# A decoder layer on one core: attention's value products for two key blocks at a time, and the last key block added to the sum by VectorE

## The reference

```python
qkv = x @ w_qkv + b_qkv                                   # self: 16 heads of 32
scores = einsum('bhqd,bhkd->bhqk', q, k) / sqrt(32)
scores = where(causal, scores, -10000.0)                  # cross: where(mask, -inf, scores)
probs = softmax(scores)
ctx = einsum('bhqk,bhkd->bhqd', probs, v)
x = x + ctx @ w_dense + b_dense
...
x = x + cross_attention(layernorm(x), ctx_1024, mask)
x = x + experts(layernorm(x))                             # argmax of 8, gelu between two 512x512 products
```

## Time and profile before

| | |
|---|---|
| Three timed runs | 1970.99, 1971.99, 1972.17 us |
| The profiled execution | span 1969.3 us (the page gives no other time of it) |
| PE busy | 1878.3 us, 95% of the span |
| PE weight loads busy | 1325.4 us, 67% |
| VectorE busy | 1349.2 us, 69% |
| ScalarE busy | 1128.1 us, 57% |
| GpSimd busy | 975.0 us, 50% |
| Mean granted TensorE clock | 0.981 |

### The profile page before, as it was taken

The page is one execution under the profiler, slowest core; times in us unless marked ns, Lnnn a source line. Parts: engine busy times, 40 slices in busy tenths (PEclk is TensorE's granted clock), DMA queues, the critical chain, the costliest instruction groups (busy, mean ns, idle before and its releaser), DMA issues. The chain is left out here.

```text
span 1969.3 us, 34918 instructions
## 1 busy us (share of the span) xinstructions
PE 1878.3 (95%) x10950; PEld 1325.4 (67%) x10950; DVE 1349.2 (69%) x2849; ACT 1128.1 (57%) x2168; POOL 975.0 (50%) x1144
## 2 busy tenths in 40 slices
PE   6999999999999999999999999999999875899997
PEld 4667777777777766666666666666666454798896
DVE  5667667676766676667676757576665476788886
ACT  3555555555555555555565656565555444688885
POOL 3455456445555555455454445554454442355454
PEclk9999999999999999999999999999999886999999
DMA  6455554645555573644444545535353456722220
GB/s 186 120 142 126 131 133 97 148 108 119 116 138 132 130 187 88 140 109 110 102 112 108 129 108 123 114 91 125 87 113 81 103 191 197 266 67 93 84 89 17
DMA packets 137658, 239.18 MB, mean 121 GB/s; under 512 B 31066, under 2 KB 32386, under 8 KB 137440
## 3 DMA queue, kind: packets, MB, share of 16 engines
q1 hardware_dynamic: 108704, 190.49, 35.5%
q0 software_dynamic: 21392, 45.37, 11.6%
q10 hardware_dynamic: 7408, 1.42, 0.4%
HBM read 114.84 MB, written 48.97 MB: 83 GB/s over the span
## 5 line engine op out<-in xcount | busy, mean ns | idle before, releaser
L558 ACT ACTIVATE attn_probs<-attn_sT 128x512 f32<-128x512 f32 (+3 forms) x1024 | 528.6, 518 | 475.8 <-PE attn_sT L872 472.8
L466 POOL TENSOR_TENSOR attn_probs<-attn_probs 128x512 f32<-128x512 f32 (+2 forms) x384 | 531.2, 1402 | 179.1 <-PE attn_o_ps L887 130.4
L667 DVE TENSOR_REDUCE attn_m_col<-attn_sS 128x1 f32<-128x512 f32 x512 | 342.7, 688 | 194.2 <-PE attn_sS L856 186.5
L872 PE MATMUL attn_sT<-attn_stack 98*128 98x512 f32 (+2 forms) x1024 | 387.1, 389 | 0.3 <-ACT attn_probs L558 0.3
L856 PE MATMUL attn_sS<-attn_stack 97*128 97x512 f32 (+2 forms) x1024 | 369.2, 371 | 14.4 <-DVE attn_m_col L667 3.3
L673 DVE CUSTOM_DVE_ANT_0 attn_sS<-attn_sS,attn_cT_low 128x128 f32<-128x128 f32 x496 | 241.1, 504 | 171.0 <-PE attn_sS L856 167.4
L872 PEld LDWEIGHTS attn_sT<-attn_stack 98*128 98x128 f32 x1024 | 188.2, 189 | 206.0 <-ACT attn_probs L558 127.8
L454 POOL TENSOR_SCALAR_AFFINE_SELECT attn_probs<-attn_probs 128x256 f32<-128x256 f32 x256 | 119.6, 467 | 345.2 <-ACT attn_probs L558 345.1
L856 PEld LDWEIGHTS attn_sS<-attn_stack 97*128 97x128 f32 x1024 | 193.5, 190 | 70.9 <-DVE attn_m_col L667 15.5
L887 PE MATMUL attn_o_ps<-attn_probs,attn_V 128*32 128x512 f32 (+3 forms) x2048 | 233.6, 527 | 5.0 <-ACT attn_probs L558 2.0
L836 PE MATMUL attn_pj<-attn_xT_high,attn_w_high 128*128 128x512 f32 x384 | 153.8, 400 | 1.4 <-DVE attn_xT_low L651 1.4
(11 more groups left out here) (212 smaller groups left out, 3703.8 us busy)
## 6 DMA issues: line engine op xcount, KB each, us to landing
attn_stack<-attn_stage SPq DMA_DIRECT2D x666, 128.0 KB, 2.3
attn_rows<-in_x_dram SPq DMA_DIRECT2D x64, 256.0 KB, 4.1
attn_rows<-x_after_self SPq DMA_DIRECT2D x64, 256.0 KB, 4.1
moe_w<-in_L_ffn_W_dram SPq DMA_DIRECT2D x16, 1024.0 KB, 15.2
attn_stack<-attn_stage POOLq DMA_DIRECT2D x96, 128.0 KB, 3.3
x_after_self<-attn_rows SPq DMA_DIRECT2D x32, 256.0 KB, 2.6
x_after_self<-in_L_attn_b_dense_dram POOLq DMA_DIRECT2D x32, 256.0 KB, 4.9
attn_rows<-in_ctx_dram SPq DMA_DIRECT2D x32, 256.0 KB, 3.0
```

What stands on the lines that cost most here:

```text
L466: pool.tensor_tensor(total, total, tile_of(n, kb)[:, js, q0:S], ALU.add).then_inc(added, 1)
L558: act.activation(tile_of(n, kb)[:, j, q0:S], sT[:, i % 2, q0:S], ACT.Exp, scale=SCALE).then_inc(exp_done, 1)
L667: dve.tensor_reduce(to, sS[:, k % 2], AX_X, ALU.max).then_inc(s_free, 1)
L872: pe.matmul(sT[:, i % 2, q0:S], stack[0:ROW_MAX + 1, n % 2, 1, j, kb * P:(kb + 1) * P], stack[0:ROW_MAX + 1, n % 2, 0, j, q0:S], start=Tru ...
```

## The change

PE multiplies probabilities by values for two key blocks in a row, blocks 0 and 1 at step 8 and blocks 2 and 3 at step 0 of the next group. The chunks are spread again: steps 4 and 12 get one, steps 13 and 14 have one instead of two, and units 1 to 3 begin one step earlier. GpSimd's adds of block 1 in self groups stand at steps 8 to 11 in place of 6, 8, 10 and 11. In self groups VectorE adds block 3 (its 128 kept columns, four heads) to the sum, in a new function `add_last_keys`, behind the first maximum of step 0; the sums' products over block 3 are left out, and the sums wait for VectorE by a new semaphore, `topped`. In cross groups the sums stay as they are.

```diff
@@ -36,7 +36,7 @@
     VRING, ORING = 5, 5
     POOL_HEAD = 3
     N_SCORES = (2, 1, 1, 2, 1, 1, 2, 1, 1, 2, 1, 1, 0, 0, 0, 0)
-    CHUNKS = ((), (0, 1), (2,), (3,), (), (4,), (5,), (6,), (), (7,), (8,), (9,), (), (10, 11), (12, 13), (14, 15))
+    CHUNKS = ((), (0, 1), (2,), (3,), (4,), (5,), (6,), (7,), (), (8,), (9,), (10,), (11,), (12,), (13,), (14, 15))
     steps = [(n, q) for n in range(-G, NG + G) for q in range(Q)]
 
     def in_batch(b):
@@ -244,7 +244,7 @@
         aux_full, aux_free = sem("aux_full"), sem("aux_free")
         s_full, s_free = sem("s_full"), sem("s_free")
         st_full, exp_done, pv_done = sem("st_full"), sem("exp_done"), sem("pv_done")
-        added, inverse_done = sem("added"), sem("inverse_done")
+        added, topped, inverse_done = sem("added"), sem("topped"), sem("inverse_done")
         refined, o_scaled = sem("refined"), sem("o_scaled")
         o_copied, o_divided, oT_high, oT_ready = sem("o_copied"), sem("o_divided"), sem("oT_high"), sem("oT_ready")
         last_full = sem("last_full")
@@ -465,7 +465,7 @@
                 total = tile_of(n, 0)[:, js, q0:S]
                 pool.tensor_tensor(total, total, tile_of(n, kb)[:, js, q0:S], ALU.add).then_inc(added, 1)
 
-            adds_at = {False: {6: ((1, 0, 1),), 8: ((1, 1, 2),), 10: ((1, 2, 3),), 11: ((1, 3, 4),), 12: ((2, 0, 2), (2, 2, 4))},
+            adds_at = {False: {8: ((1, 0, 1),), 9: ((1, 1, 2),), 10: ((1, 2, 3),), 11: ((1, 3, 4),), 12: ((2, 0, 2), (2, 2, 4))},
                        True: {8: ((1, 0, 1), (1, 1, 2), (1, 2, 3), (1, 3, 4)), 12: ((2, 0, 2), (2, 2, 4))}}
 
             def add_bias(b, t):
@@ -686,6 +686,14 @@
                 dve.wait_ge(inverse_done, 2 * n + 2)
                 dve.tensor_tensor(extra[:], extra[:], rec[:], ALU.mult).then_inc(refined, 1)
 
+            def add_last_keys(n):
+                dve.wait_ge(exp_done, Q * (n + 1))
+                dve.wait_ge(masked, 2 * NB * (n + 1))
+                dve.wait_ge(added, adds_before(n + 1))
+                cols = slice(from_q(n, NB - 1), S)
+                total = tile_of(n, 0)[:, :, cols]
+                dve.tensor_tensor(total, total, tile_of(n, NB - 1)[:, :, cols], ALU.add).then_inc(topped, 1)
+
             def divide(n):
                 dve.wait_ge(o_copied, n + 1)
                 dve.wait_ge(inverse_done, 2 * n + 2)
@@ -755,6 +763,8 @@
                 if n != FIRST_CROSS - 3:
                     for key in found[:1]:
                         maximum(key)
+                if q == 0 and in_groups(n - 1) and not is_cross(n - 1):
+                    add_last_keys(n - 1)
                 if q == 2 and in_groups(n - 1):
                     divide(n - 1)
                 if q == 3 and in_groups(n - 1):
@@ -891,12 +901,15 @@
             def sums(n):
                 begin_aux(("den", n))
                 pe.wait_ge(added, adds_before(n + 1))
-                q0 = from_q(n, NB - 1)
+                if not is_cross(n):
+                    pe.wait_ge(topped, n + 1)
                 for j in range(J):
-                    pe.matmul(extra[HD * j:HD * (j + 1), :], ones[:], tile_of(n, 0)[:, j], start=True, stop=False)
-                for j in range(J):
-                    op = pe.matmul(extra[HD * j:HD * (j + 1), q0:S], ones[:], tile_of(n, NB - 1)[:, j, q0:S],
-                                   start=False, stop=True)
+                    op = pe.matmul(extra[HD * j:HD * (j + 1), :], ones[:], tile_of(n, 0)[:, j],
+                                   start=True, stop=not is_cross(n))
+                if is_cross(n):
+                    for j in range(J):
+                        op = pe.matmul(extra[HD * j:HD * (j + 1), :], ones[:], tile_of(n, NB - 1)[:, j],
+                                       start=False, stop=True)
                 op.then_inc(aux_full, 1)
 
             def last_chunk(t, k):
@@ -939,10 +952,11 @@
                     scores(key)
                 for u, k in parts[1:]:
                     chunk(u, k)
-                if q % J == 0:
-                    of, kb = (n, q // J - 1) if q else (n - 1, NB - 1)
+                if q in (0, Q // 2):
+                    of, blocks = (n, (0, 1)) if q else (n - 1, (2, 3))
                     if in_groups(of):
-                        weighted_values(of, kb)
+                        for kb in blocks:
+                            weighted_values(of, kb)
                         if q == 0:
                             sums(of)
                 if in_groups(n) and q == 0:
```

## The result

The changed kernel takes 2045.31 us (median of four runs, 2039.12 to 2046.45) against 1972.08 us before: ratio 1.0368, 95% interval 1.0354 to 1.0382, **73 us slower**. The prediction said slower by 26 and named 2018 as the upper end. The profiled execution is the one of 2039.12 us, with a span of 2037.4 us, 68.1 more than before.

The account below looks back on a forecast made before the run. PE was taken to set the pace. Costs of 80.8 us against 55.0 saved gave +25.8, a span of 1995.1 and, with 2.7 added, 1997.8, said as 1998 us; range 1948 to 2018, likeliest case 1975 to 2018.

Parts of the forecast that it names:

- The gain, 55: PE time removed: fewer excursions into 32-column products 44.8, block 3 sums 6.7, mask wait 3.5, together 55.0 us.
- Step 4 to 7, 25.1: PE gets ahead of VectorE and waits at step 7's score for a free bank: 25.1 us lost.
- First self groups, 18.4: At the group's end PE waits 2.3 us for VectorE's added add before the sums, x 8 = 18.4 us.
- Second self groups, 8.8: The fourth turn waits for turned rows queued behind the output's low part on VectorE: 1.1 x 8 = 8.8 us.
- Third and fourth self groups, 7.2: Before the sums PE waits for VectorE's add, 0.29 to 0.6 us a group: 0.45 x 16 = 7.2 us.
- No DMA is added: Listed among the hidden effects: the change adds no DMA; no time was charged for it.
- third and fourth cross groups have slack: The output's low part, delayed by GpSimd's adds, was said not to matter there; no time charged.
- First cross groups, 8.0: The last output-projection chunk at step 15 waits 0 to 2.0 us for the output's low part: 1.0 x 8 = 8.0 us.
- Second cross groups, 13.3: The fourth turn waits 0.9 to 2.8 us for turned rows behind the output's low part: 1.9 x 7 = 13.3 us.
- no step turns on the clock: With the granted clock at 1.00 and 0.99 in the attention groups, no step of the forecast depended on it.
- The new add: VectorE's add of block 3 behind step 0's first maximum in self groups takes 0.69 us; the sums wait for it.
- Rival 1: The cover holds and VectorE catches up; only step 7 and 0.29 us waits charged: 25.3 gained, 1947 us, chance 0.16.

Follow-up runs that it names:

- run 5: The changed kernel with the keys' half emptied at step 6 and VectorE's part at 7, in place of 4 and 5: 2017.14 us, ratio 1.0225.
- run 6: The changed kernel with the queries' half emptied at steps 8 and 9 in place of 10 and 11: 2027.2 us, ratio 1.027.
- run 4: The changed kernel with the output split at steps 7 and 8 in place of 12 and 13, third groups as they were: 2013.03 us, ratio 1.0199.
- run 1: The changed kernel without VectorE's add, the sums again taking block 3 by products in self groups: 2029.59 us, ratio 1.0296.
- run 2: The kernel before with VectorE's add and single sums in self groups, products and chunks at their old places: 1997.99 us, ratio 1.0133.
- run 8: The changed kernel, add kept, with output split at steps 7 and 8, keys' half at 6 and 7, queries' half at 8 and 9: 1959.77 us, ratio 0.9951.
- run 7: The changed kernel without the add, output split at steps 7 and 8, keys' half at 6 and 7, queries' half at 8 and 9: 1950.28 us, ratio 0.9887.
- run 9: The kernel before with only the output split at steps 7 and 8 and the keys' half emptied at 6 and 7: 1988.36 us, ratio 1.0074.

## Why the prediction was wrong

Its sign and mechanism held; its size did not, and one step was false.

- **The gain, 55.** Right within 4 us. Steps 4 and 5 are 0.53 and 0.50 us shorter (0.51 and 0.50 were worked out), PV0 ahead of PV1 costs 0.84, and the mask wait at step 8 is gone in third and fourth self groups (0.68 to 0.70 in place of 0.84). By the table some 51 us.
- **Step 4 to 7, 25.1.** Right: 0.47 x 32 + 0.49 x 24 + 0.22 x 8 = 28.5; run 5 takes it away. One reading was rough: of the 32 waits of the weight load put down to step 7, 25 stand there.
- **First self groups, 18.4.** Right in size: 2.4 us a group against 2.3, though 0.59 of it stands at the output projection. **Second self groups, 8.8**: 1.1 us as said.
- **Third and fourth self groups, 7.2.** Measured 0.95 us a group, twice the 0.45. The add's part is 0.6, the upper end of its bounds; the other 0.33 goes with the rows (run 6).
- **"No DMA is added" and "third and fourth cross groups have slack".** This is the step that failed. No DMA was added, but one chain of DMAs lost its cover. The prediction followed each engine's queue past the moved steps and took a transfer that nobody waits for (2.8 us in all before) as one without cost. It never measured how long that chain is, nor how much PE work lay over it. From the low half to the score it is 4.0 to 5.3 us. PE's waits for it went from 2.8 to 21.4 us, and run 6, which starts it earlier, gets 18 us back. First, third and fourth cross groups and third and fourth self groups meet it: 0.9 and 0.6 us in third and fourth cross groups, where zero stood, 0.7 to 1.1 us in first cross groups in three of the six inner batches, and 0.3 us in the self groups.
- **First cross groups, 8.0.** 0.6 us a group in place of 1.0, so near by luck and for another reason, the rows: the low part takes 0.87 us here, and the split moved away in run 4 leaves the end at +1.44. The Trainium skill's rule (SBUF — State Buffer, Who interferes with whom), by which this term would have been zero, agrees with that.
- **Second cross groups, 13.3.** The term mis-sized most: 3.7 us a group in place of 1.9. The turn comes 2.4 us later, inside the bounds of 0.9 and 2.8, and 0.3 more goes at the scores behind it. The other 0.9, in five of seven groups, is the low clock, for which the prediction had no term; it said that no step turns on the clock.
- **The new add.** Its own 0.69 us was right (0.71 in the row above). By runs 1, 2 and 8 it costs 16, 26 and 9.5 to 13 us net, in spite of 6.7 saved, so of the two parts of the change this one loses in every setting tried.

Against the sum: step 7 is 3 us over, self groups' ends 9 over, cross groups' ends 25 over (46 against 21.3), the gain 4 under. That is 41 of the 47 us by which it was short. Most of the rest is the distance between the profiled run and the median: 6.2 us after the change, 1.1 before.

Rival 1 (1947) has a time close to that of run 7 (1950), but by accident: the rival charges 25.1 us at step 7 and keeps the add, and run 7 has neither. With step 7 hidden as well its own terms give 1922 (1917 hides the add's wait too). It was the wrong forecast for this kernel, since every chain kept its old start; with earlier starts about half of what PE saves came out as time, 22 of 48 us.

## What to carry to other kernels

When work is taken off the engine that sets the pace, every chain that ran under it loses that much cover, those that nobody waits for today too: list the chains that end at each later meeting point, DMAs included, with their length from the first instruction to the last landing, and compare each with what is left of the cover. Here a VectorE instruction that came to stand beside GpSimd's long run of adds held up its whole queue, and a wait of the pacing engine went with a slower clock. Then move the starts of the chains together with the work: the pairs without the add were 58 us slower with the old starts (run 1) and 22 us faster with three starts moved (run 7).

## What the runs showed of the hardware

- Seven waits of PE of 2.19 to 2.22 us at the same place, in second cross groups: with five of them the granted clock fell from 1.00 to 0.50 for about 3.4 us, at 0.3 us before to 1.1 us after the end of the wait; with two it stayed at 1.00. The groups with the fall are 0.9 us longer. With the same seven waits it fell five times in run 1, six times in run 6 and once in run 5. With the wait taken away by an edit on VectorE's and ScalarE's order alone (run 4), the clock is 1.00 at all seven places. Which other idle times would do it was not tried.
- VectorE's instruction with two inputs in SBUF took between 0.74 and 3.42 us by what GpSimd did. It ended 0.54 us after the adds that it met (1273.94 against 1273.40), and in run 9 it was held over two adds with a mask of the causal kind between them (433.65 to 437.07, the second add ending at 436.51), though by its recorded start it came 0.25 us ahead of the first. By the recorded starts the one that issued first did not go first here; GpSimd's recorded starts are rough, so the true order is open.
- The way from VectorE's last half to a score through four DMAs was 4.0 us long in one third cross group and 5.3 us in the next batch's: 0.4 to 0.6 us for each issue, and 1.6 and 2.9 us from the end of the last issue to the product.
